# Moving the turn of the attention heads, and the loads of Q, in an adaLN block with routed experts

## The reference

```python
h = _layernorm(x, axis=-1) * (1 + ca) + sa
x = x + ga * _L0_attn_ref(h, Wq, Wk, Wv)      # 16 heads of 8, one K and one V for all heads
h = _layernorm(x, axis=-1) * (1 + cb) + sb
x = x + gb * _L0_ffn_ref(h, router_w, w1, b1, w2, b2)   # 8 experts, 2 per token, F = 512, gelu
```

## Time and profile before

| | us |
|---|---|
| median of three timed runs | 608.9 |
| the profiled execution's own time | 614.37 |
| its span, first to last instruction | 612.6 |
| TensorE matmuls busy in the span | 544.6 (89%) |
| VectorE busy | 503.6 (82%) |
| ScalarE busy | 435.9 (71%) |
| GpSimd busy | 306.5 (50%) |
| mean granted TensorE clock | 0.960 of full speed |

### The profile page before, as it was taken

The page is one execution under the profiler, slowest core; times in us unless marked ns, Lnnn a source line. Parts: engine busy times, 40 slices in busy tenths (PEclk is TensorE's granted clock), DMA queues, the critical chain, the costliest instruction groups (busy, mean ns, idle before and its releaser), DMA issues.

```text
span 612.6 us, 21006 instructions
## 1 busy us (share of the span) xinstructions
PE 544.6 (89%) x7675; PEld 337.3 (55%) x7675; DVE 503.6 (82%) x1190; ACT 435.9 (71%) x724; POOL 306.5 (50%) x581
## 2 busy tenths in 40 slices
PE   2669999999999999999999999968886896999970
PEld 2222345555555545545545545425876885999960
DVE  5878999999999899899899899876564673755697
ACT  5674588889888889889888888768443432566661
POOL 2615010134475676675775766760555465455470
PEclk9888999999999999999999999989997998899995
DMA  6289500220310410401401401111322122232645
GB/s 191 64 275 353 137 8 13 52 59 10 76 42 23 103 33 24 115 23 28 112 23 27 116 18 28 28 41 42 84 71 65 57 73 74 76 86 60 202 139 176
DMA packets 54484, 49.44 MB, mean 81 GB/s; under 512 B 20224, under 2 KB 48944, under 8 KB 53664
## 3 DMA queue, kind: packets, MB, share of 16 engines
q1 hardware_dynamic: 46864, 36.89, 22.4%
q0 software_dynamic: 4320, 9.38, 4.7%
q10 hardware_dynamic: 3200, 1.84, 1.0%
HBM read 29.40 MB, written 17.10 MB: 76 GB/s over the span
## 4 chain that ended last, share of the span: by engine, by line
PE 55%; DVE 15%; POOL 6%; issue 6%; another core or an unknown queue 5%; DMA 4%; SPq 3%; ACT 3%; DVEq 1%; POOLq 0%; ACTq 0%
PE ps L1052 13%; PE ps L1068 12%; PE ps L1079 12%; DVE neg_max L1364 7%; PE ps L1162 7%; PE ps L1151 7%; DMA Q<-max_parts 3%; POOL h_sorted L812 2%; ACT parts L1291 1%; PE ps L1142 1%; PE ps L1109 1%; DVE P L286 1%; SPq L948 1%; PE ps L1116 1%
## 5 line engine op out<-in xcount | busy, mean ns | idle before, releaser
L1364 DVE TENSOR_REDUCE neg_max<-ps 128x1 f32<-128x512 f32 x512 | 322.3, 681 | 19.3 <-PE ps L1052 15.9
L1252 ACT ACTIVATE P<-ps,zero 128x1024 f32<-128x1024 f32 x256 | 280.1, 1117 | 52.5 <-PE ps L1068 45.4
L1052 PE MATMUL ps<-K,Q 128*32 128x512 bf16 x2048 | 196.4, 382 | 4.3 <-DVE neg_max L1364 3.6
L1068 PE MATMUL ps<-Q,K 128*32 128x512 bf16 x2048 | 156.5, 381 | 5.7 <-ACT P L1252 3.6
L1079 PE MATMUL ps<-P,V 128*32 128x256 f32 x2048 | 157.8, 382 | 0.5 <-ACT P L1252 0.4
L1602 POOL DMA_INDIRECT y_rows<-P,to_now x71 | 72.2, 1017 | 87.5 <-DVE P L1427 46.0
L1291 ACT ACTIVATE parts<-ps,parts 128x128 f32<-128x128 f32 x228 | 63.8, 381 | 61.0 <-remote 23.7
L1052 PEld LDWEIGHTS ps<-K,Q 128*32 128x32 bf16 x2048 | 55.0, 96 | 74.7 <-DVE neg_max L1364 28.8
L1079 PEld LDWEIGHTS ps<-P,V 128*32 128x32 f32 x2048 | 61.9, 110 | 48.7 <-issue 3.0
L1068 PEld LDWEIGHTS ps<-Q,K 128*32 128x32 bf16 x2048 | 53.9, 97 | 61.1 <-ACT P L1252 11.6
L812 POOL DMA_INDIRECT h_sorted<-diag,slot x64 | 65.8, 1028 | 33.7 <-POOL max_parts L79 16.5
(11 more groups left out here) (241 smaller groups left out, 542.9 us busy)
## 6 DMA issues: line engine op xcount, KB each, us to landing
Q<-q_parts SPq DMA_DIRECT2D x24, 384.0 KB
xs<-h_sorted SPq DMA_DIRECT2D x71, 72.0 KB
W<-w_t SPq DMA_DIRECT2D x2, 2048.0 KB, 11.0
q_parts<-parts SPq DMA_DIRECT2D x8, 384.0 KB, 3.7
Q<-y_rows SPq DMA_DIRECT2D x6, 512.0 KB
diag<-att_u SPq DMA_DIRECT2D x128, 16.0 KB
Q<-max_parts SPq DMA_DIRECT2D x96, 4.0 KB
out<-Q SPq DMA_DIRECT2D x6, 256.0 KB, 2.8
```

The source lines that it names most:

```text
L1052: ins = eng.matmul(ring_bank(*unit)[QUAD * q:QUAD * (q + 1), :], Q[buffer_of(g)][:, g % NG * G + q, at:at + QUAD], K[buffer_of(g)][:, 0, : ...
L1068: ins = eng.matmul(to, K[p][:, 1, at:at + QUAD], Q[p][:, first:first + 2, some], start=True, stop=True, tile_position=(0, QUAD * q))
L1252: nc.scalar.activation(P[s % 2][:, :, HALF * u:HALF * (u + 1)], bank(2 * u, 2).rearrange("p (j t) -> p j t", j=G), ACT.Exp, bias=zero[:], ...
L1364: eng.tensor_reduce(neg_max[g % 2][:, at:at + 1], ring_bank("maximum", g, s, j), AX.X, ALU.max, negate=True).then_inc(ring_used, 1)
```

## The change

In the ring's order and on TensorE, the turn of the heads (`turn_heads`) of the batch that ended moves from step 1, place 3 to step 2, place 1 of the same group. So the ring's order there goes from sums, maximum, maximum, heads, ranks, maximum, maximum to sums, maximum, maximum, ranks, maximum, maximum, heads. ScalarE's `heads_out` moves from ahead of the exponential (s = 2, u = 0) to ahead of (s = 2, u = 1). The title of the change calls this the turn of the heads' sums; the turn of the softmax sums itself stays where it is.

`load_operands` is split in `load_queries` (three DMAs of 384 KB) and `load_others` (six of K, one of V), which also changes their order in the queue from Q, K, K three times and V to three Q, six K and V. In a refill group, SP now first waits until all scores of the groups before g are done, issues the three loads of Q, and only then does `shift(g + 1)` and `regroup(g - 1)`; K and V follow behind these, behind the wait on the values as before.

```diff
-        def load_operands(eng, b, p, loaded, begin=0, end=3):
-            for blk in range(begin, end):
+        def load_operands(eng, b, p, loaded):
+            load_queries(eng, b, p, loaded)
+            load_others(eng, b, p, loaded)
+
+        def load_queries(eng, b, p, loaded):
+            for blk in range(3):
                 rows = slice(QUAD * blk, QUAD * blk + 3 * DK)
                 eng.dma_start(Q[p][rows, :, :]...).then_inc(loaded[p], 16)
+
+        def load_others(eng, b, p, loaded):
+            for blk in range(3):
+                rows = slice(QUAD * blk, QUAD * blk + 3 * DK)
                 for n in (0, 1):
                     eng.dma_start(K[p][rows, n, :]...).then_inc(loaded[p], 16)
-            if begin == 0:
-                eng.dma_start(V[p][:]..., v_cols[b]).then_inc(loaded[p], 16)
+            eng.dma_start(V[p][:]..., v_cols[b]).then_inc(loaded[p], 16)
...
# ring_order, and the same condition in TensorE's loop
-                        if s == 1 and j == 3 and batch_at(g, 1) is not None:
+                        if s == 2 and j == 1 and batch_at(g, 1) is not None:
                             units.append(("heads turned", batch_at(g, 1)))
...
# SP
                 for g in range(GROUPS):
                     b = g // NG + 1
+                    refill = g % NG == 0 and 2 <= b < B
+                    if refill:
+                        eng.wait_ge(score_done, START + g * T * 2)
+                        load_queries(eng, b, b % 2, batch_loaded)
                     if g + 1 < GROUPS:
                         shift(g + 1)
                     if 0 < g < GROUPS - 1:
                         regroup(g - 1)
-                    if g % NG == 0 and 2 <= b < B:
+                    if refill:
                         eng.wait_ge(pv_done, START + g * T * 2)
-                        load_operands(eng, b, b % 2, batch_loaded)
+                        load_others(eng, b, b % 2, batch_loaded)
...
# ScalarE
-                            if s == 2 and u == 0 and batch_at(g, 1) is not None:
+                            if s == 2 and u == 1 and batch_at(g, 1) is not None:
                                 heads_out(batch_at(g, 1))
```

More of the change, by code:

```diff
@@ L154, in load_operands @@
                                   ).then_inc(loaded[p], 16)
-            if begin == 0:
-                eng.dma_start(V[p][:].rearrange("p t c -> p (t c)"), v_cols[b]).then_inc(loaded[p], 16)
+            eng.dma_start(V[p][:].rearrange("p t c -> p (t c)"), v_cols[b]).then_inc(loaded[p], 16)
         def variances(own, tiles, mean, var):
@@ L1007, in _ @@
                 eng.wait_ge(cleared, START + 8)
-                load_operands(eng, 1, 1, batch_loaded, 0, 3)
+                load_operands(eng, 1, 1, batch_loaded)
                 eng.wait_ge(row_out, START + B)
```

## The result

The changed kernel takes 615.39 us (median of 4 runs, 613.19 to 616.86) beside 609.22 for the kernel before on the same chip (4 runs): a ratio of 1.0109, 95% interval 1.0073 to 1.0146. It is slower by 6.2 us. The forecast was 609.1 (range 606.8 to 611.8), and slower had a chance of 0.28. From the first scores of group 0 to those of group 31 the two traces have 343.4 and 349.0 us: +5.6, nearly all of the loss. Up to group 30 the granted clock is 1.00 in both; over group 30 it is 0.88 before and 0.77 after, and that group alone has 0.6 of the 5.6.

The account below looks back on a forecast made before the run. TensorE was taken to set the pace in the attention loop, with VectorE near its limit. Terms +1.5 - 1.4 - 0.4 + 0.3 = 0.0 us on the 608.9 median, rounded up by 0.2 to 609.1; range 606.8 to 611.8.

Parts of the forecast that it names:

- Step 3, cost: Refills: the shift, now behind Q's three loads, would land late in group 5 only, by 0 to 0.75 us; +0.3 taken.
- rival A: First scores of groups 5, 9, ... 25 wait for the shift behind Q: 615.5 us, or 612 at half that lateness; chance 0.15.
- need-sum: Refills: time from a group's last scores until Q and the shift have landed, 10.6 to 12.4 us, against 12.71 or 11.65.
- tail: Refills: the shift's landing behind Q's loads, estimated at 0.3 to 1.2 us.
- Step 3, gain: Groups 6 and 14: shifts land in time once Q leaves earlier; 0.32 in the first pair plus 0.1, -0.4 us in sum.
- Step 1: TensorE's turns: ranks parted from heads add 0.30 us in each of groups 9, 13, 17, 21, 25, +1.5 us in sum.
- Step 2: VectorE, fed more evenly at the turns, loses less time: 0.35 us for each of four pairs of groups, -1.4 us.
- rival C: VectorE's 1.17 us idling at the turn is not from the turn and stays: +1.4 us, 610.3 us; chance 0.17.
- the two turns at 1.02: Sign in TensorE's chain: turns of ranks and heads would together cost 1.07 us, with 0.14 or so behind the ranks.
- VectorE's idling under 0.8: Sign at the turns: VectorE's longest idle time would fall below 0.8 us, from 1.17.
- no shift waited for in groups 6 and 14: Sign in the refills' waits: no "DMA Q<-max_parts" in groups 6 and 14.
- the stall in group 5 only: Sign in the refills' waits: one wait for the shift, of 0 to 0.75 us, in group 5 and nowhere else.

Follow-up runs that it names:

- first comparison: The whole change against the kernel before, both on a chip of the slower kind: 615.39 us beside 609.22, ratio 1.0109.
- the control: The kernel before, unchanged, timed against itself on a chip of the faster kind: ratio 0.9996, loop 336.2 us.

## Why the prediction was wrong

**Step 3, cost: the step that failed.** The sum that set the shift's landing against its deadline said that it fits in every refill but the first. I had 0 to 0.75 us of stall in group 5 only and took 0.3; the traces have 2.8 us in six refills (first comparison) and 2.7 (faster kind), and rival A's mechanism in all six. The need-sum's terms for the refill of group 12: Q's first packet at 196.59 (my 194.21 + 0.66 + 0.04 + 1.4 = 196.3), its last at 205.63, 9.0 us (my 8.2 to 9.1), and the shift down at 207.90, 2.3 us behind (my 0.3 to 1.2). The tail is the mis-sized term: 1.1 to 2.3 us in the six. With it the sum is 13.4 where 12.7 were there. Only the refill of group 8 is late by its drain instead: 10.2 us, for 8.5 to 9.0 in the other five, and a tail of 1.1. I had read the tail as the distance between two landings of the old order, the batch's and the shift's; from Q's last packet it is longer, by what a landing takes. The packets show its parts. The shift has 192 of 64 bytes: 96 start from 200.45 to 201.98, in the midst of Q's, the other 96 between 204.58 and 206.00, when Q's are nearly through; the landing is 1.9 us behind the last of them (1.8 in the same refill on the faster kind, 1.4 with two loads ahead). Most of the time eight of Q's packets are under way at once in this refill, half of 16 (share 0.54 in the earlier trace rows). The trace doesn't name the engine of a packet, but this reads as if the engines without Q carried half of the shift in time, and the wait was for the other half. The Trainium skill, DMA: Bandwidth & Descriptors, Queues, rings and completion order, has a ring taken in order on each engine; the landings 0.04 ahead of six first scores, and the waits of some 4 us for the regroup behind Q, agree. I had cited it, found nothing against A in it, and still gave A 0.15. A's time, 615.5, stands beside the measured 615.39 by luck: it has 6.5 us of stalls in it, and 2.8 came.

**Step 3, gain.** 0.4 forecast; 0.31 in group 5 came (11.86 to 11.55). It can be larger than one profile shows: in the control the old place costs 1.7 us in group 13, and one or two loads ahead gain 1.3 to 1.4 us of time.

**Step 1** had the right sign and nearly the size: +0.30 a turn forecast, 0.25 in group 17's chain (ranks 0.15 + 0.14, heads 0.59 + 0.14: 1.02 for 0.77), 0.24 on the faster kind. Group 29 was called covered; on the faster kind 0.14 of its 0.25 is.

**Step 2** is not shown; there is room for about half of it. With two loads ahead on the slower kind the groups 5 to 26 of the turn and the statistics have 133.70 us for the 134.04 of before, with 1.2 of parting in them: 1.5 back, of which 0.32 in group 5 and 0.4 in group 13 are the loads'. That leaves some 0.8 for VectorE, of 1.4 forecast. Two loads ahead with everything else in place was not run on the slower kind, so it isn't known what of the 0.8 the moved heads make. On the faster kind there are no such waits to remove, and the heads' move is parting alone, as rival C had it in its sum.

**The sum.** Of the signs that I had named, the two turns at 1.02, VectorE's idling under 0.8 and no shift waited for in groups 6 and 14 all came; the stall in group 5 only did not. The forecast was 609.1, in effect a ratio of 1.000; the change with two loads ahead has 1.0011. So steps 1 and 2 and the gain of step 3 came out right as a sum, and the third load ahead, late six times and with what that drags, makes the step from 1.0011 to 1.0082. One thing in the first profile no step or rival names: groups 15, 23 and 27 last 11.60 to 11.68 for 11.10 to 11.19, with a route of GpSimd starting on a unit of scores. In the second on the same kind only group 15 does (11.60). What sets that phase stays open, and so does why the change costs 0.003 to 0.005 more on the slower kind of chip. It is not shown that routes cause it.

## What to carry to other kernels

A large load put ahead of a small urgent one on the same queue cost, here, the whole drain plus the small one's own landing; take both from a trace where nothing lies between them, and move only as much of the load as the deadline has room for (here two of three blocks: 0.998 for 1.005). List every transfer that ends up behind it, each with its own deadline: the regroup cost ten times what the shift did (35 us for 3 to 4), more than a quarter of it by the clock that fell behind TensorE's standstill. And before an input of an in-order engine is moved, look at the last thing that engine does in the round, not at the first.

## What was not expected of the hardware

The same kernel takes 586 us in three comparisons, on three chips, and 609 to 611 in two others. Of the 28.8 us between the two profiles of the kernel before, 7.3 lie in the loop (336.2 and 343.4 us) and 20 behind it, at a granted clock of 0.94 and 0.92:

```profile
401.00:583.80 182.80, 154.67 (x1387) 143.87 (x1387) 131.73 (x444) 106.17 (x336) 100.62 (x104) 0.94 0.36 103
```

```profile
410.00:612.60 202.60, 161.65 (x1387) 148.01 (x1387) 129.90 (x437) 104.61 (x337) 95.46 (x97) 0.92 0.32 92
```

(Windows from the loop's end to the end of the span: bounds, length, busy PE, PEld, DVE, ACT, POOL, then clock, DMA share, GB/s; the kernel before on the faster and on the slower kind.) What the traces of the two kinds differ in is one sort of wait, for which the profile finds no releaser on the core ("remote"). In the loop of the kernel before, on the slower kind:

```profile
ACT P L1252 <- remote: 4.6, 2, 2.6
```

Both are in group 30. Behind them the clock falls there too (0.88 over that group, 1.00 on the faster kind), and the group lasts 14.47 us for 9.92, 4.5 of the loop's 7.3. Behind the loop the same trace has 31.9 us of such waits of ScalarE, the longest 9.0, and 20.5 of VectorE. All six profiles of the slower kind have them, 3.1 to 4.7 us in the loop and 18 to 32 us of ScalarE's behind it; none of the twelve of the faster kind has one. What ScalarE waits for there was not studied. It matters for the reading: waits of 0.1 to 0.5 us in the group behind a turn were seen, with the ranks in their place, on the slower kind only (groups 18, 22 and 26), and a term built on them, as step 2, is one of that kind.
